# Two rounding passes of a requantisation loop moved from VectorE to GpSimd

## The chip, the cores and the metric

The kernel runs on all 8 cores of one Trainium2 chip. The metric is device time in microseconds of the slowest core. Each core computes 2 of the 16 batch rows with the same program, and nothing is exchanged between cores. In the profile the engines are PE (TensorE), DVE (VectorE), ACT (ScalarE), POOL (GpSimd) and SP (SyncE).

## The reference

The input x is [16, 2048, 1024] in float32. It is normalised over the last axis; one branch is a causal linear attention with decay, the other a quantised feed-forward block, and their product is added to x.

```
xn = layernorm(x)
s  = attention(xn)                       # q, k, v, o of width 256, decayed causal scores
h  = act_quant(xn) @ weight_quant(w1).T  # 1024 -> 4096
h  = silu(depthwise_conv1d(h, conv_w, conv_b))       # 3 taps along the sequence
y  = act_quant(h) @ weight_quant(w2).T   # 4096 -> 1024
out = x + s * silu(y)

def act_quant(x):
    scale = 127.0 / clip(max(abs(x), axis=-1), 1e-5)
    return clip(round(x * scale), -128, 127) / scale
```

The change is in act_quant(h), in its x * scale and round.

## The kernel before

**Set-up.** A core loads and quantises both weight matrices once (wquant) and keeps them in SBUF: w1q in bf16, w2q in f16. Then it goes through its 2 batch rows. In each, the 2048 positions are cut into 8 groups of GT = 256, taken from the last to the first.

**A group.** For each half of 128 positions stageA normalises, transposes and quantises the input, and stageB does the attention step. stageC multiplies the group by w1 into hs0 or hs1 (32 channel chunks of 128 partitions x 256 positions, f16). After that, tail of the group one later runs, since the convolution needs its neighbour. So tail runs 8 times in a batch row and 16 times on a core.

**The tail.** It is written in this order: (a) the convolution as small matmuls into psC and psD, with Silu on ACT back into hs (L744, L755); (b) a max tree and a min tree over the channels on DVE (L766 to L777), and per-position scales from them (L788 to L812); (c) the scales are spread over all partitions by two matmuls into psG (L827); (d) the requantisation loop, `for q in range(HC // 2)`, of 16 passes over two channel chunks each (128 x 512 elements); (e) for each half tl, 64 matmuls by w2 into psE and psF (L875), Silu on ACT, the attention output, the product with it, the sum with x, and one output DMA issued from POOL's queue (L963).

**A pass of loop (d)** has four DVE instructions. L837 multiplies hs by the scales in psG into scrf. L843 adds and subtracts 1.5 x 2^23 from scrf into g_sb. L847 adds and subtracts 1.5 x 2^52 on scrf in place. L851 forms g_sb * col(29) + scrf into hs. The constant col(29), worked out once from the engine's own arithmetic, makes the last step pick whichever of the two roundings is a real one. There is one buffer scrf and one buffer g_sb. The q loop names no other engine.

**Order and waits.** Each engine has its own queue, in the order in which the program is written. E.op increments a counter semaphore of its engine (V for DVE, G for POOL, T for PE, S for ACT) at each instruction. The program is built with strict=True: ahead of each instruction, an engine other than PE waits for its own counter to reach the number it has issued, so that an instruction starts only when the one before it has ended. Waits already made are not repeated:

```
            if (self.strict and self.ownsem is not None
                    and self.which != "tensor"):
                v0 = self.n.get(self.ownsem, 0)
                if v0 > 0 and v0 > self.waited.get(self.ownsem, 0):
                    self.eng.wait_ge(self.sems[self.ownsem], v0)
```

The first matmul behind the loop waits for its last DVE instruction, vhq:

```
                w = (use("psE0") + use("psE1h") + use("psF") + [("V", vhq)] +
                     [res.get("colsB", ("V", 0))])
```

Of the kernel before, what the change touches and what calls it, by code (L numbers as in the profile page):

```python
# [12 lines left out]
ALU = mybir.AluOpType  # L13
# [99 lines left out]
def build_nc(S=S_FULL, nbatch=NB_BATCH, strict=True, detect_races=False, limit=None):  # L113
# [102 lines left out]
    def col(i):  # L216
        return cols[:, i:i + 1]

    def schedule(E: Emit):
        n = E.n  # L220
        res = {}

        def use(key):
            return [res[key]] if key in res else []
# [7 lines left out]
        def hwaits(b):  # L232
            return [res[k] for k in
                    ("hs%d_T" % b, "hs%d_V" % b, "hs%d_S" % b) if k in res]
# [24 lines left out]
        def hap(kb, c0, nch, w=GT, off=1):  # L259
            a = hsb[kb][:, c0 * HSW + off: c0 * HSW + off + nch * HSW]  # L260
            return a.rearrange("p (a q) -> p a q", a=nch, q=HSW)[:, :, 0:w]
# [41 lines left out]
        for dst, src in casts:  # L303
            E.op("vector", lambda v, d=dst, s=src: v.tensor_copy(out=d, in_=s),
                 waits=[("DC", dc_all)])
        if "convdiag" not in DBG_SKIP:
            for idx in range(96):
# [3 lines left out]
                    waits=[("DC", dc_all)])  # L311
# [4 lines left out]
            waits=[("DC", dc_all)])  # L316
        E.op("vector", lambda v: v.tensor_scalar(
            out=col(28), in0=col(28), scalar1=2.0 ** 30, scalar2=None,
            op0=ALU.mult))
        E.op("vector", lambda v: v.tensor_scalar(  # L320
            out=col(29), in0=col(28), scalar1=-1.0, scalar2=1.0,
            op0=ALU.mult, op1=ALU.add))
        E.op("scalar", lambda s: s.activation(
            out=scal[0:1, 2:3], in_=scal[0:1, 0:1], func=AF.Sigmoid),
            waits=[("DC", dc_all)])
# [12 lines left out]
        for slot in (LND, DCN, OSC):  # L338
# [10 lines left out]
            waits=[("V", v_bc)])  # L349
# [383 lines left out]
        def tail(bi, k, base):  # L733
# [3 lines left out]
            for hc in range(HC):  # L737
                pb = hc % 2
                w = use("psCD%d" % pb) + (wh if hc == 0 else [])
                for i in range(4):  # L740
                    for kk in range(3):
# [11 lines left out]
                             waits=(w if (kk == 0 and i == 0) else []))  # L753
# [5 lines left out]
                    waits=[("T", tcv)] + (wh if hc <= 1 else []))  # L759
# [5 lines left out]
            for op2, base2 in ((ALU.max, 0), (ALU.min, 1)):  # L765
# [3 lines left out]
                    waits=(wtree if base2 == 0 else []))  # L769
# [11 lines left out]
                for tl in range(2):  # L781
                    sl = transp(scr[:, tl * 128:(tl + 1) * 128], bf="f16",
                                waits=[("V", vtree)])
# [3 lines left out]
                    if base2 == 0:  # L787
# [3 lines left out]
                            waits=[("T", ttr)] + use("colsB"))  # L791
                    else:
# [16 lines left out]
                            op0=ALU.mult, op1=ALU.mult))  # L809
# [11 lines left out]
            for t2 in range(2):  # L821
# [3 lines left out]
                    waits=[("V", vrbcols)] + use("dgt"))  # L825
# [4 lines left out]
                    waits=[("V", vdg2)] + use("psG%d" % (slb + t2)))  # L830
# [4 lines left out]
            for q in range(HC // 2):  # L835
                c0 = q * 2
                E.op("vector", lambda v, c2=c0, rp=rb_ps: v.tensor_tensor(  # L837
                    out=scr_f32[:, 0:512].rearrange(
                        "p (a q2) -> p a q2", a=2, q2=GT),
                    in0=hap(kb, c2, 2),  # L840
                    in1=rp.unsqueeze(1).broadcast_to([128, 2, GT]),
                    op=ALU.mult), waits=(wrd if q == 0 else []))
                E.op("vector", lambda v: v.tensor_scalar(  # L843
                    out=g_sb[:, 0:512], in0=scr_f32[:, 0:512],
                    scalar1=12582912.0, scalar2=12582912.0,
                    op0=ALU.add, op1=ALU.subtract))
                E.op("vector", lambda v: v.tensor_scalar(  # L847
                    out=scr_f32[:, 0:512], in0=scr_f32[:, 0:512],
                    scalar1=6755399441055744.0, scalar2=6755399441055744.0,
                    op0=ALU.add, op1=ALU.subtract))  # L850
                E.op("vector", lambda v, c2=c0: v.scalar_tensor_tensor(  # L851
                    out=hap(kb, c2, 2),
                    in0=g_sb[:, 0:512].rearrange(
                        "p (a q2) -> p a q2", a=2, q2=GT),
                    scalar=col(29),
                    in1=scr_f32[:, 0:512].rearrange(
                        "p (a q2) -> p a q2", a=2, q2=GT),
                    op0=ALU.mult, op1=ALU.add))
            res["gx"] = ("V", n["V"])
            setr("scrf", "V")  # L860
            vhq = n["V"]
# [7 lines left out]
            for tl in range(2):  # L869
                w = (use("psE0") + use("psE1h") + use("psF") + [("V", vhq)] +  # L870
                     [res.get("colsB", ("V", 0))])
                for hc in range(HC):
                    for dgrp, p2 in ((0, psE), (1, psF)):
# [8 lines left out]
                             waits=(w if (hc == 0 and dgrp == 0) else []))  # L882
                tf2 = n["T"]
                htouch(kb, "T")
                for dgrp, p2 in ((0, psE), (1, psF)):
# [5 lines left out]
                         waits=[("T", tf2), ("V", vhq)] +  # L891
# [8 lines left out]
                for i in range(2):  # L900
# [8 lines left out]
                         waits=[("T", trt)])  # L909
# [4 lines left out]
                for cc in range(2):  # L914
# [7 lines left out]
                         waits=(w if cc == 0 else []))  # L922
# [4 lines left out]
                    waits=[("T", tu)] + use("u_sb"))  # L927
# [7 lines left out]
                    waits=[("T", tut)] + use("uT_sb"))  # L935
# [3 lines left out]
                for dgrp, p2 in ((0, psE), (1, psF)):  # L939
# [25 lines left out]
                    waits=[("V", vcb)], inc=do, amt=16)  # L965
            res["xg%d" % kb] = ("DO%d" % kb, n["DO%d" % kb])

        for bi in range(nbatch):
            base = bi * S
            E.op("vector", lambda v: v.memset(S_sb[:, :], 0.0),  # L970
                 waits=use("S_sb"))
# [5 lines left out]
            for g0 in (NG - 1, NG - 2):  # L977
                if g0 < 0:
# [8 lines left out]
                    waits=use("xg%d" % bidx), inc=dx, amt=16)  # L987
                setr("xg%d" % bidx, dx)

            for g in range(NG - 1, -1, -1):  # L990
# [26 lines left out]
                if "SCOL" not in DBG_SKIP:  # L1017
                    vsc = n["V"]
                    for tl in range(2):
# [3 lines left out]
                            waits=use("dgt"))  # L1023
# [5 lines left out]
                            waits=[("V", vdg)] +  # L1029
# [5 lines left out]
                        waits=[("T", tscb)] + use("scol_sb"))  # L1035
# [4 lines left out]
                if g <= NG - 2:  # L1040
                    oth = (g + 1) % 2
                    wf = hwaits(cur) + hwaits(oth)
                    E.op("vector", lambda v, o=oth, c=cur: v.tensor_copy(
                        out=hsb[o][:, 0:HC * HSW:HSW],
                        in_=hsb[c][:, GT:HC * HSW:HSW]), waits=wf)
                    E.op("vector", lambda v, o=oth, c=cur: v.tensor_copy(
                        out=hsb[c][:, GT + 1:HC * HSW:HSW],
                        in_=hsb[o][:, 1:HC * HSW:HSW]))
                    htouch(cur, "V")
                    htouch(oth, "V")  # L1050
                    if "TAIL" not in DBG_SKIP:
                        tail(bi, g + 1, base)
                if 1 <= g <= NG - 2:
# [8 lines left out]
                        waits=use("xg%d" % bidx), inc=dx, amt=16)  # L1062
                    setr("xg%d" % bidx, dx)
            E.op("vector", lambda v: v.memset(hs0[:, 0:HC * HSW:HSW], 0.0),
                 waits=hwaits(0))
            htouch(0, "V")
            if "TAIL" not in DBG_SKIP:
                tail(bi, 0, base)
# [50 lines left out]
```

How the kernel before makes its waits and increments, by code:

```python
    def op(self, engine, fn, waits=(), inc=None, amt=1, serialize=False):  # L47
        if inc is None:
            inc = ENG2SEM[engine]
        self.total += 1
        if self.limit is not None and self.total > self.limit:
            self.n[inc] += amt
            return self.n[inc]
        if engine == "tensor" and (serialize or self.tser):
            if engine == self.which:
                v0 = self.n["T"]
                if v0 > 0 and v0 > self.waited.get("T", 0):
                    self.eng.wait_ge(self.sems["T"], v0)
                    self.waited["T"] = v0
            self.tser = serialize
        if engine == self.which:
            if (self.strict and self.ownsem is not None
                    and self.which != "tensor"):
                v0 = self.n.get(self.ownsem, 0)
                if v0 > 0 and v0 > self.waited.get(self.ownsem, 0):
                    self.eng.wait_ge(self.sems[self.ownsem], v0)
                    self.waited[self.ownsem] = v0
            for sk, v in waits:
                if v > 0 and v > self.waited.get(sk, 0):
                    self.eng.wait_ge(self.sems[sk], v)
                    self.waited[sk] = v
            inst = fn(self.eng)
            inst.then_inc(self.sems[inc], amt)
        self.n[inc] += amt
        return self.n[inc]
```

## Time and profile before

| | |
|---|---|
| median of 3 runs | 5139.29 us (5133.31 to 5140.38) |
| the profiled execution | 5140.66 us |
| its span, slowest core | 5139.1 us (the eight cores: 5122.6 to 5139.1) |
| PE busy | 1950.4 us (38%) |
| DVE busy | 2324.1 us (45%) |
| ACT busy | 402.8 us (8%) |
| POOL busy | 17.3 us (0%), 36 instructions |

No engine is busy for half of the span. A share of busy time therefore tells little here, and the stages have to be read one by one in the order of time. The span is that of the traced instructions on the slowest core; the device time of the same execution is 1.6 us more.

### The profile page before, as it was taken

What the parts mean: (1) busy time and instruction counts of PE and PEld (TensorE: products, weight loads), DVE (VectorE), ACT (ScalarE), POOL (GpSimd) and SP (SyncE); (2) the same over time, 40 slices, a digit from 0 to 9 for tenths busy, and PEclk for the clock granted to TensorE, in tenths of its full rate; (3) what the DMA queues carried; (4) which work ended last, traced back from release to release, by engine and by line L of the source; (5) the groups of instructions that cost most, each with busy time, mean ns of one, the idle gap of its engine ahead of it and who ended that gap; (6) DMA issues with size and microseconds to landing.
All of it is one profiled execution on the core that took longest, in us unless ns stands there. A gap on an engine that the chain in (4) does not pass through costs nothing.

```text
span 5139.1 us, 45903 instructions; the slowest of 8 cores (5122.6 to 5139.1 us)
## 1 busy us (share of the span) xinstructions
PE 1950.4 (38%) x14474; PEld 1178.8 (23%) x14474; DVE 2324.1 (45%) x5416; ACT 402.8 (8%) x745; POOL 17.3 (0%) x36
## 2 busy tenths in 40 slices
PE   0000015536253433345354356353443444353543
PEld 0000003314131222223132134131222223131311
DVE  4875764343534343534334543444343434434344
ACT  0000000101001010101011001001010101010110
POOL 0000000000000000000000000000000000000000
PEclk9999997666667575766676666667575767676766
DMA  4323210000000000000000000000000000000000
GB/s 129 104 93 106 72 51 1 1 17 1 17 1 5 13 1 17 1 17 1 17 1 17 17 1 1 17 1 5 13 1 17 1 17 1 17 1 17 1 9 9
DMA packets 43507, 105.54 MB, mean 21 GB/s; under 512 B 12292, under 2 KB 14468, under 8 KB 39172
## 3 DMA queue, kind: packets, MB, share of 16 engines
q1 hardware_dynamic: 38660, 85.82, 5.1%
q0 software_dynamic: 4608, 16.78, 0.8%
q8 instruction: 120, 1.97, 0.2%
q14 instruction: 119, 0.97, 0.1%
HBM read 85.80 MB, written 16.78 MB: 20 GB/s over the span
## 4 chain that ended last, share of the span: by engine, by line
DVE 41%; PE 37%; issue 11%; DMA 5%; ACT 3%; DVEq 2%; SPq 0%; ACTq 0%; POOL 0%; POOLq 0%
PE psG L254 8%; PE psE L875 5%; PE psF L875 5%; PE psA L703 5%; PE psB L703 5%; DVE sb_scr L771 4%; DVE sb_hs L851 4%; DVE sb_scrf L837 3%; PE psC L744 3%; DVE sb_g_sb L843 2%; DVE sb_scrf L847 2%; ACT sb_hs L755 2%; PE psD L744 2%; DVE sb_xg L430 2%; DMA sb_xg<-w2t 2%
## 5 line engine op out<-in xcount | busy, mean ns | idle before, releaser
L254 PE MATMUL psG<-sb_eyef,sb_g_sb 128*128 128x128 f32 x1024 | 392.4, 487 | 1211.3 <-ACT sb_g_sb L493 744.6
L875 PE MATMUL psE<-sb_w2q,sb_hs 128*128 128x512 f16 x1024 | 426.7, 417 | 730.1 <-DVE sb_hs L851 700.6
L254 PEld LDWEIGHTS psG<-sb_eyef,sb_g_sb 128*128 128x128 f32 x1024 | 256.6, 312 | 1351.9 <-issue 1351.9
L875 PE MATMUL psF<-sb_w2q,sb_hs 128*128 128x512 f16 x1024 | 424.8, 415 | 0.0
L875 PEld LDWEIGHTS psE<-sb_w2q,sb_hs 128*128 128x128 f16 x1024 | 108.3, 106 | 884.7 <-issue 786.9
L703 PE MATMUL psA<-sb_xqsT,sb_w1q 128*128 128x256 bf16 x2048 | 270.4, 290 | 0.0
L703 PE MATMUL psB<-sb_xqsT,sb_w1q 128*128 128x256 bf16 x2048 | 254.9, 280 | 0.0
L905 DVE CAST sb_Rg<-psG 128x128 bf16<-128x128 f32 x64 | 18.6, 291 | 513.9 <-PE psG L254 513.9
L703 PEld LDWEIGHTS psA<-sb_xqsT,sb_w1q 128*128 128x128 bf16 x2048 | 213.8, 104 | 34.7
L703 PEld LDWEIGHTS psB<-sb_xqsT,sb_w1q 128*128 128x128 bf16 x2048 | 206.7, 101 | 29.4
L771 DVE TENSOR_TENSOR sb_scr<-sb_scr,sb_hs 128x512 f16<-128x512 f16 x448 | 191.8, 428 | 47.8 <-DVE sb_scr L771 0.9
L766 DVE TENSOR_TENSOR sb_scr<-sb_hs 128x512 f16<-128x512 f16 x32 | 13.7, 428 | 429.9 <-ACT sb_hs L755 428.3
L851 DVE SCALAR_TENSOR_TENSOR sb_hs<-sb_g_sb,sb_cols,sb_scrf 128x512 f16<-128x512 f32 x256 | 193.1, 754 | 27.0 <-DVE sb_scrf L847 0.5
L744 PE MATMUL psC<-sb_hs,sb_convdiag 32*32 32x256 f16 x3072 | 162.8, 313 | 108.2 <-ACT sb_hs L755 72.5
L837 DVE TENSOR_TENSOR sb_scrf<-sb_hs,psG 128x512 f32<-128x512 f16 x256 | 175.8, 687 | 42.1 <-PE psG L827 16.3
L561 DVE CAST sb_xqsT<-psG 128x128 bf16<-128x128 f32 x256 | 74.7, 292 | 262.2 <-PE psG L254 262.2
L515 DVE CAST sb_xqsT<-psG 128x128 bf16<-128x128 f32 x256 | 74.7, 292 | 234.5 <-PE psG L254 229.0
L744 PE MATMUL psD<-sb_hs,sb_convdiag 32*32 32x256 f16 x3072 | 164.2, 314 | 17.4 <-ACT sb_hs L755 1.9
L755 ACT ACTIVATE sb_hs<-psC,sb_convb_sb 128x256 f16<-128x256 f32 x256 | 122.1, 477 | 603.3 <-PE psD L744 578.6
L392 PE MATMUL psG<-sb_cols,sb_onem 128*128 128x1 f32 x4 | 1.1, 348 | 440.6 <-DVE sb_cols L388 440.6
L721 DVE TENSOR_TENSOR sb_hs<-psA,sb_scol_sb 128x512 f16<-128x512 f32 x128 | 88.8, 694 | 164.4 <-PE psB L703 125.5
L887 ACT ACTIVATE sb_g_sb<-psE,sb_cols 128x512 f32<-128x512 f32 x32 | 22.0, 687 | 1692.5 <-PE psG L254 1692.5
(150 smaller groups left out, 2466.0 us busy)
## 6 DMA issues: line engine op xcount, KB each, us to landing
sb_xg<-w1t SPq DMA_DIRECT2D x32, 1024.0 KB, 5.3
sb_xg<-w2t SPq DMA_DIRECT2D x128, 256.0 KB, 2.6
sb_xg<-x SPq DMA_DIRECT2D x16, 1024.0 KB, 4.9
out<-sb_xg POOLq DMA_DIRECT2D x32, 512.0 KB, 2.9
sb_xg<-basis SPq DMA_DIRECT2D x1, 512.0 KB
sb_xg<-basisT SPq DMA_DIRECT2D x1, 512.0 KB
sb_xg<-qcT SPq DMA_DIRECT2D x1, 128.0 KB
sb_xg<-kcT SPq DMA_DIRECT2D x1, 128.0 KB
```

The costliest lines, as they stand in the source:

```text
L254: t.matmul(out=psG[:, s * 128:(s + 1) * 128], lhsT=a, rhs=idn[:, :], start=True, stop=True),
L430: v.scalar_tensor_tensor(out=f[:, s3], in0=scrf[:, 0:512], scalar=col(29), in1=f[:, s3], op0=ALU.mult, op1=ALU.add))
L703: lambda t, i2=i, h2=hc, p2=pb, s2=slot: t.matmul(out=psAB[p2][:, s2:s2 + 256], lhsT=w1q[:, i2 * H + h2 * 128: i2 * H + (h2 + 1) * 128], r ...
L721: v.tensor_tensor(out=d, in0=s3, in1=s4, op=ALU.mult),
L744: t.matmul(out=psCD[p2][32 * i2:32 * (i2 + 1), 0:256], lhsT=convdiag[32 * i2:32 * (i2 + 1), (h2 * 3 + k2) * 32: (h2 * 3 + k2 + 1) * 32], r ...
L755: E.op("scalar", lambda s, h2=hc, p2=pb: s.activation(out=hk[:, h2 * HSW + 1:h2 * HSW + 1 + GT], in_=psCD[p2][:, 0:256], func=AF.Silu, bia ...
L771: E.op("vector", lambda v, c2=c0, o3=op2: v.tensor_tensor(out=scr[:, 0:512].rearrange("p (a q) -> p a q", a=2, q=GT), in0=scr[:, 0:512].re ...
L837: E.op("vector", lambda v, c2=c0, rp=rb_ps: v.tensor_tensor(out=scr_f32[:, 0:512].rearrange("p (a q2) -> p a q2", a=2, q2=GT), in0=hap(kb, ...
L843: E.op("vector", lambda v: v.tensor_scalar(out=g_sb[:, 0:512], in0=scr_f32[:, 0:512], scalar1=12582912.0, scalar2=12582912.0, op0=ALU.add, ...
L847: E.op("vector", lambda v: v.tensor_scalar(out=scr_f32[:, 0:512], in0=scr_f32[:, 0:512], scalar1=6755399441055744.0, scalar2=6755399441055 ...
L851: E.op("vector", lambda v, c2=c0: v.scalar_tensor_tensor(out=hap(kb, c2, 2), in0=g_sb[:, 0:512].rearrange("p (a q2) -> p a q2", a=2, q2=GT ...
L875: lambda t, h2=hc, d2=dgrp, t2=tl, p3=p2: t.matmul(out=p3[:, 0:512], lhsT=hk[:, h2 * HSW + 1 + t2 * 128: h2 * HSW + 1 + (t2 + 1) * 128], r ...
```

## The change

In each pass of loop (d), the two rounding instructions L843 and L847 are issued on GpSimd with the same operands and constants. The first of them waits for the multiplication by DVE, and DVE's last instruction of the pass waits for the second.

```diff
+                vq1 = n["V"]
-                E.op("vector", lambda v: v.tensor_scalar(
+                E.op("gpsimd", lambda g: g.tensor_scalar(
                     out=g_sb[:, 0:512], in0=scr_f32[:, 0:512],
                     scalar1=12582912.0, scalar2=12582912.0,
-                    op0=ALU.add, op1=ALU.subtract))
-                E.op("vector", lambda v: v.tensor_scalar(
+                    op0=ALU.add, op1=ALU.subtract), waits=[("V", vq1)])
+                E.op("gpsimd", lambda g: g.tensor_scalar(
                     out=scr_f32[:, 0:512], in0=scr_f32[:, 0:512],
                     scalar1=6755399441055744.0, scalar2=6755399441055744.0,
                     op0=ALU.add, op1=ALU.subtract))
-                E.op("vector", lambda v, c2=c0: v.scalar_tensor_tensor(
+                gq = n["G"]
+                E.op("vector", lambda v, c2=c0, gq2=gq: v.scalar_tensor_tensor(
                     out=hap(kb, c2, 2),
                     ...
-                    op0=ALU.mult, op1=ALU.add))
+                    op0=ALU.mult, op1=ALU.add), waits=[("G", gq)])
```

## Rows read from the trace of the kernel before

**Rows 1.** Spans and granted TensorE clock of the cores and dies.

```profile
core 0: 5139.1 us, clock 0.703
core 3: 5122.6 us, clock 0.709
...
die 0 (median of its cores): 5127.2 us, clock 0.709
die 1 (median of its cores): 5129.5 us, clock 0.708
```

**Rows 2.** Waits: engine, line, releaser; us in total, times, longest us.

```profile
PE psE L875 <- DVE sb_hs L851: 700.6, 16, 44.0
```

**Rows 3.** Instruction groups of loop (d): count, busy us, mean ns, idle before.

```profile
L851 DVE SCALAR_TENSOR_TENSOR sb_hs<-sb_g_sb,sb_cols,sb_scrf 128x512 f16<-128x512 f32 x256 | 193.1, 754 | 27.0 <-DVE sb_scrf L847 0.5
...
L837 DVE TENSOR_TENSOR sb_scrf<-sb_hs,psG 128x512 f32<-128x512 f16 x256 | 175.8, 687 | 42.1 <-PE psG L827 16.3 <-DVE sb_hs L851 0.9
L843 DVE TENSOR_SCALAR sb_g_sb<-sb_scrf 128x512 f32<-128x512 f32 x256 | 109.3, 427 | 28.3 <-DVE sb_scrf L837 1.4
L847 DVE TENSOR_SCALAR sb_scrf<-sb_scrf 128x512 f32<-128x512 f32 x256 | 109.2, 427 | 27.9 <-DVE sb_g_sb L843 0.9
```

**Rows 4.** Timeline of the first tail: start us, duration us.

```profile
1029.98 0.69 DVE L837 TENSOR_TENSOR sb_scrf<-sb_hs,psG 128x512 f32<-128x512 f16 x1 [1.02 <-PE psG L827]
1030.78 0.43 DVE L843 TENSOR_SCALAR sb_g_sb<-sb_scrf 128x512 f32<-128x512 f32 x1
1031.31 0.43 DVE L847 TENSOR_SCALAR sb_scrf<-sb_scrf 128x512 f32<-128x512 f32 x1
1031.84 0.75 DVE L851 SCALAR_TENSOR_TENSOR sb_hs<-sb_g_sb,sb_cols,sb_scrf 128x512 f16<-128x512 f32 x1
1032.70 0.69 DVE L837 TENSOR_TENSOR sb_scrf<-sb_hs,psG 128x512 f32<-128x512 f16 x1
...
1072.59 0.75 DVE L851 SCALAR_TENSOR_TENSOR sb_hs<-sb_g_sb,sb_cols,sb_scrf 128x512 f16<-128x512 f32 x1
...
1073.49 0.58 PE L875 MATMUL psE<-sb_w2q,sb_hs 128*128 128x512 f16 x1 [43.61 <-DVE sb_hs L851]
```

**Rows 5.** Windows: the first tail's loop, and the matmuls behind it.

```profile
1030.00:1073.40 43.40, 0.00 (x0) 0.00 (x0) 36.70 (x64) 0.00 (x0) 0.00 (x0) 0.50 0.00 0
...
1074.00:1076.00 2.00, 2.00 (x6) 0.61 (x5) 0.00 (x0) 0.00 (x0) 0.00 (x0) 0.50 0.03 8
```

**Rows 6.** One-input passes at other rates, and the DVE's shortest, same columns as rows 3.

```profile
L379 DVE TENSOR_REDUCE sb_scrf<-sb_xg 128x4 f32<-128x512 f32 x64 | 43.9, 686 | 55.3 <-DMA sb_xg<-w2t 54.6 <-DVE sb_cols L388 0.5 <-DVE sb_cols L367 0.2
...
L489 DVE TENSOR_SCALAR sb_cols<-sb_cols 128x1 f32<-128x1 f32 x32 | 4.9, 153 | 3.4
...
L887 ACT ACTIVATE sb_g_sb<-psE,sb_cols 128x512 f32<-128x512 f32 x32 | 22.0, 687 | 1692.5 <-PE psG L254 1692.5
```

**Rows 7.** All groups of POOL.

```profile
L963 POOL DMA_DIRECT2D out<-sb_xg x32 | 17.1, 536 | 5115.9 <-DVE sb_xg L955 5075.2 <-DVE sb_hs L1064 40.7
...
L116 POOL MEMSET const-float32-1.0<- 128x1 f32 x1 | 0.1, 98 | 0.0
```

**Rows 8.** Timeline around one output DMA at the end of a tail.

```profile
1116.74 1.23 DVE L955 TENSOR_TENSOR sb_xg<-sb_xg,sb_g_sb 128x1024 f32<-128x1024 f32 x1
1118.54 0.53 POOL L963 DMA_DIRECT2D out<-sb_xg  x1 [21.98 <-DVE sb_xg L955]
```

## The prediction

> **What bounds the kernel now.** I read the spans of the cores first. The two dies lie 2.3 us apart at nearly one clock, so the execution is undisturbed and core 0, the slowest, can stand for the time [rows 1]. On the page no engine is busy for half of the span, so no engine's total decides, and the next view is that of the waits. There TensorE's first matmul by w2 (L875) waits 16 times for the last instruction of the requantisation loop, 700.6 us in total, the longest wait being 44.0 us [rows 2]. Sixteen is the number of tails on a core; the loop stands once in each with PE idle behind it.
>
> The next question is whether anything else works during that wait. The window over the first tail's loop has 64 DVE instructions and none on PE, ACT or POOL, and the DMA share is 0.00 [rows 5]. The 64 are 16 passes of four. So the loop is a stretch in which one instruction at a time runs on the whole core, and the timeline shows them end to end: L837, L843, L847, L851, and L837 again [rows 4]. The 15 passes between the L851 at 1031.84 and that at 1072.59 take 40.75 us, 2.717 us each. The four durations add up to 687 + 427 + 427 + 754 = 2295 ns [rows 3], which leaves 0.422 us for four starts, 0.105 us each. That gap is the wait of each instruction for the end of the one ahead. All 256 passes look alike: L843 and L847 have 256 instructions each at a mean of 427 ns [rows 3], and 256 passes of 2.717 us are 695 us, of the 700.6 us that PE waits [rows 2]. Everything that a pass gains or loses arrives at the end of the kernel 256 times.
>
> **The change part by part.** Removed from DVE: L843 and L847, 256 instructions each of 427 ns, with a 0.105 us start ahead of each. That is 2 x (0.427 + 0.105) = 1.064 us of a pass, or 272 us in all. If DVE were the bound beside a working POOL, these could be hidden. They are not: L843 reads what L837 of the same pass has just written, L851 needs both results, and the next L837 comes behind L851 in DVE's queue and overwrites scrf. With one scrf and one g_sb, POOL's two instructions lie exactly where DVE's two lay, and DVE stands idle meanwhile. The gain by taking work off DVE is nothing: the price is the difference between the two engines' times for the same two instructions, plus the difference in the starts.
>
> Added on the path: two TENSOR_SCALAR on POOL, of 128x512 f32 in and out, with duration P each; a start of POOL behind DVE; a start of POOL behind itself (strict order makes the second wait for the first to end); and a start of DVE behind POOL.
>
> *The duration P.* POOL computes nothing in this trace but four 128x1 MEMSETs of about 98 ns, and issues 32 DMAs at 536 ns [rows 7]. P must come from neighbours. The lower bound is built from fixed cost and rate. DVE's shortest TENSOR_SCALAR takes 153 ns, which leaves 274 ns of the 427 for 512 elements, 0.54 ns each [rows 3, 6]. POOL's smallest instruction of 98 ns [rows 7] with that same rate gives 98 + 274 = 372 ns. DVE evidently runs this shape in a fast way, since passes over as many elements elsewhere take much longer: 686 ns for a reduction with one input on DVE, 687 ns for an activation on ACT [rows 6], and 754 ns for L851 with two operations and two inputs [rows 3]. For the upper bound I take twice the ordinary pass, 2 x 686 = 1372 ns, on the grounds that rows of 128x512 within this trace differ by a factor of 1.8 (427 to 754) and POOL could lie as far again beyond the ordinary row. I choose 754 ns, the row nearest in kind: 512 float32 elements, two arithmetic operations, no fast way. The difference is 2 x (754 - 427) = 654 ns per pass, 167 us in all.
>
> The trace has no POOL arithmetic with which to judge a page's figure. The Trainium skill (GPSIMD Engine Reference, section 3.1, Elementwise — side-by-side cycle accounting) puts a tight POOL loop at about 1.8 cycles per element and gives 769 ns for 512 elements. By that figure the term would be 2 x (769 - 427) = 684 ns per pass, 175 us, and the total estimate 8 us higher than mine.
>
> *The starts.* Among DVE's own instructions a start is 0.105 us, and from the last L851 (ends at 1073.34) to the first matmul (1073.49) it is 0.15 us [rows 4]. POOL was slower in the one thing that it does here: DVE's sum ended at 1117.97 and POOL's DMA began at 1118.54, 0.57 us later [rows 8]. For each of POOL's two starts the bounds are therefore 0.105 and 0.57 us. The DMA's start may contain preparation that an arithmetic instruction hasn't, so I don't charge 0.57 twice. I charge it for the start behind DVE, which is the same kind of hand-over, and 0.105 us for POOL's start behind itself, because its MEMSET row shows a small fixed cost [rows 7]. DVE's start behind POOL I also take at 0.105 us, as behind itself. The extra is 0.57 - 0.105 = 0.465 us per pass, 119 us in all.
>
> *What else moves.* POOL's queue holds the output DMAs too. The last DMA of a tail is issued before the next tail's loop begins, and the convolution and both trees of that tail lie between; issuing a DMA takes 536 ns and is long done by then, so it costs nothing [rows 7]. Inside the loop no transfer is under way (DMA share 0.00), so nothing contends, and DVE and POOL never run together. TensorE has the lower clock, 0.50 of full speed or 1.2 GHz, during the loop and in the first 2 us behind it already [rows 5]. A longer idle time can't lower it further, and I cost that at nothing.
>
> **Sum.** 256 x (0.654 + 0.465) = 256 x 1.119 = 286 us. The profiled execution took 5140.7 us (span 5139.1 and 1.6 around it), 1.4 us above the median of the runs. 5140.7 + 286 = 5427 us, and 5425 us by the median. That is slower by 5.6%.
>
> **The rivals.**
>
> *A, POOL keeps DVE's rate.* P is then 427 ns. With the start of 0.57 us behind DVE the price is 256 x 0.465 = 119 us, or 5259 us; with ordinary starts it is 0, and the time stays at 5140 us. For it: nothing says that the same arithmetic must be slow on another engine. Against it: 427 ns is the exception among the rows of 512 elements [rows 3, 6]. The page of the skill that speaks for it is GPSIMD Engine Reference, section 4.1, Engine selection, which calls one-input elementwise work on POOL roughly line rate; no row here tests that.
>
> *B, POOL is a slow engine for arithmetic.* P is 1100 to 1372 ns and both starts are 0.57 us. At the upper ends: 2 x (1372 - 427) + 2 x 465 = 2820 ns per pass, 722 us, or 5862 us. At 1100 ns with one slow start: 1346 + 465 = 1811 ns, 464 us, or 5604 us. For it: POOL's only hand-over shown is five times an ordinary one [rows 8]. Against it: its MEMSET takes only 98 ns [rows 7].
>
> *C, faster than before.* If POOL has the fixed cost of its MEMSET and DVE's fast rate, P is 372 ns; with ordinary starts the gain is 256 x 2 x 0.055 = 28 us, or 5112 us. It decides when P plus the mean POOL start falls below 0.532 us. Against it stands the start of 0.57 us [rows 8], which alone is more than that.
>
> *D, the change doesn't do what it says,* in that DVE goes on with other work while POOL rounds. That would need the next L837 to run ahead, which the queue and the single scrf exclude; I give it no chance.
>
> **How the numbers follow.** The forecast, P of 600 to 1000 ns with one slow start or both half slow, spans 5300 to 5560 us and has 0.62. A between 5150 and 5300 us has 0.17. B above 5560 us has 0.15. No change has 0.04 and C 0.02. Two in ten may lie outside the range: it reaches down into A to 5230 and up into B to 5620 us. About 0.2% (10 us) is what a measurement of this kernel can tell from no change. Faster by more than that has 0.02, within it 0.04, slower 0.94.
>
> **What would show each step.** In the profile after, the wait of psE L875 for L851 should grow from 700.6 us to about 987 us over the same 16 times. Each pass should take 3.84 us. L837 and L851 should keep 687 and 754 ns, and POOL should have 512 TENSOR_SCALAR of about 754 ns, with DVE's idle time ahead of L851 at about 2.3 us per pass (0.57 + 0.754 + 0.105 + 0.754 + 0.105). DVE's busy time should fall by 218 us to about 2106 us while the kernel gets longer. PE's groups should keep their durations. The prediction is wrong if P or the starts are off: an error of 100 ns in P moves the time by 51 us, one of 100 ns in one start by 26 us. It is wrong in kind if the extra per pass is right but the total isn't, since then the loop isn't bare, or if L837 or L851 change their own durations.

## The result and the profile after

| | before | after |
|---|---|---|
| median of 8 runs each | 5138.12 us | 5932.72 us |
| lowest to highest | 5133.31 to 5144.83 | 5929.25 to 5934.66 |
| profiled execution, span of its slowest core | 5139.1 us | 5929.0 us |
| DVE busy | 2324.1 us | 2106.0 us |
| POOL busy | 17.3 us | 1002.1 us |

The ratio is 1.1546, with a 95% interval of 1.1533 to 1.1559: the changed kernel is 794.6 us slower. The forecast was 5425 us with a range of 5230 to 5620. The sign was right and the size was not, since the loss is 2.8 times as large as the 286 us that I had.

The waits of the changed kernel (engine, line, what it waited for; us in total, times, longest us) answer to [rows 2]:

```profile
PE psE L877 <- DVE sb_hs L853: 1491.3, 16, 93.7
DVE sb_hs L853 <- POOL sb_scrf L848: 1092.4, 256, 4.6
```

TensorE waits the same 16 times at the same place, 1491.3 us in place of 700.6. That difference of 790.7 us is the whole loss: the two profiled executions lie 5929.0 - 5139.1 = 789.9 us apart, the medians 794.6 us. Inside the loop DVE now waits in each of its 256 passes for POOL's second instruction.

The groups of instructions of the loop answer to [rows 3]:

```profile
L848 POOL TENSOR_SCALAR sb_scrf<-sb_scrf 128x512 f32<-128x512 f32 x256 | 492.0, 1922 | 40.2 <-POOL sb_g_sb L844 40.2
L844 POOL TENSOR_SCALAR sb_g_sb<-sb_scrf 128x512 f32<-128x512 f32 x256 | 491.9, 1922 | 4158.2 <-DVE sb_scrf L837 4158.2
...
L853 DVE SCALAR_TENSOR_TENSOR sb_hs<-sb_g_sb,sb_cols,sb_scrf 128x512 f16<-128x512 f32 x256 | 193.0, 754 | 1092.4 <-POOL sb_scrf L848 1092.4
...
L837 DVE TENSOR_TENSOR sb_scrf<-sb_hs,psG 128x512 f32<-128x512 f16 x256 | 176.0, 688 | 42.1 <-PE psG L827 16.4
```

The two DVE instructions that stayed have kept 688 and 754 ns. POOL's two take 1922 ns each, 4.5 times DVE's 427. The timeline of one pass (start us, duration us; it answers to [rows 4]) shows how they stand:

```profile
1033.45 0.69 DVE L837 TENSOR_TENSOR sb_scrf<-sb_hs,psG 128x512 f32<-128x512 f16 x1
1034.30 1.92 POOL L844 TENSOR_SCALAR sb_g_sb<-sb_scrf 128x512 f32<-128x512 f32 x1 [1.80 <-DVE sb_scrf L837]
1036.37 1.92 POOL L848 TENSOR_SCALAR sb_scrf<-sb_scrf 128x512 f32<-128x512 f32 x1 [0.15 <-POOL sb_g_sb L844]
1038.40 0.75 DVE L853 SCALAR_TENSOR_TENSOR sb_hs<-sb_g_sb,sb_cols,sb_scrf 128x512 f16<-128x512 f32 x1 [4.26 <-POOL sb_scrf L848]
1039.26 0.69 DVE L837 TENSOR_TENSOR sb_scrf<-sb_hs,psG 128x512 f32<-128x512 f16 x1
```

A pass takes 1039.26 - 1033.45 = 5.81 us in place of 2.717. POOL starts 0.16 us after DVE's multiplication has ended, 0.15 us after its own first instruction, and DVE starts 0.11 us after POOL. So nearly all of the 3.09 us that a pass has gained is duration: 2 x (1.922 - 0.427) = 2.99 us. The window over the first loop has PE at rest and its granted clock at 0.50, the lower level, as before, only for twice as long (the columns are those of [rows 5]: the window and its length, then busy us and instructions of PE, PEld, DVE, ACT and POOL, then PE's clock, DMA share and GB/s):

```profile
1028.40:1120.40 92.00, 0.00 (x0) 0.00 (x0) 22.37 (x31) 0.00 (x0) 61.51 (x32) 0.50 0.00 0
```

### The profile page after: what moved, and what is told of

Read it like the earlier page. It is cut to its first block, busy times and chain, and to the rows that moved or that the text cites. A ratio compares the mean times of both kernels' runs of the same rounds, so it can differ in the third digit from the quotient of the medians.

```text
span 5929.0 us, 46383 instructions; the slowest of 8 cores (5916.3 to 5929.0 us)
## 1 busy us (share of the span) xinstructions
PE 1927.2 (33%) x14442; PEld 1171.8 (20%) x14474; DVE 2106.0 (36%) x4904; ACT 402.8 (7%) x745; POOL 1002.1 (17%) x548
## 4 chain that ended last, share of the span: by engine, by line
DVE 32%; PE 31%; POOL 17%; issue 11%; DMA 4%; ACT 3%; DVEq 2%; POOLq 0%; SPq 0%; ACTq 0%
POOL sb_scrf L848 8%; POOL sb_g_sb L844 8%; PE psG L254 7%; PE psE L877 4%; PE psF L877 4%; PE psA L703 4%; PE psB L703 4%; DVE sb_scr L771 3%; DVE sb_hs L853 3%; DVE sb_scrf L837 3%; PE psC L744 2%; ACT sb_hs L755 2%; PE psD L744 2%; DVE sb_xg L430 2%; DMA sb_xg<-w2t 1%
## 5 line engine op out<-in xcount | busy, mean ns | idle before, releaser
L844 POOL TENSOR_SCALAR sb_g_sb<-sb_scrf 128x512 f32<-128x512 f32 x256 | 491.9, 1922 | 4158.2 <-DVE sb_scrf L837 4158.2
L877 PE MATMUL psE<-sb_w2q,sb_hs 128*128 128x512 f16 x1024 | 428.1, 418 | 1520.1 <-DVE sb_hs L853 1491.3
L254 PE MATMUL psG<-sb_eyef,sb_g_sb 128*128 128x128 f32 x1024 | 392.5, 487 | 1218.8 <-ACT sb_g_sb L493 753.6
L254 PEld LDWEIGHTS psG<-sb_eyef,sb_g_sb 128*128 128x128 f32 x1024 | 256.7, 312 | 1359.4 <-issue 1359.4
L848 POOL TENSOR_SCALAR sb_scrf<-sb_scrf 128x512 f32<-128x512 f32 x256 | 492.0, 1922 | 40.2 <-POOL sb_g_sb L844 40.2
L744 PE MATMUL psC<-sb_hs,sb_convdiag 32*32 32x256 f16 x3072 | 154.3, 299 | 111.7 <-ACT sb_hs L755 80.0
L744 PE MATMUL psD<-sb_hs,sb_convdiag 32*32 32x256 f16 x3072 | 155.0, 299 | 21.5 <-ACT sb_hs L755 5.8
```

The costliest lines, as they stand in the source:

```text
L254: t.matmul(out=psG[:, s * 128:(s + 1) * 128], lhsT=a, rhs=idn[:, :], start=True, stop=True),
L744: t.matmul(out=psCD[p2][32 * i2:32 * (i2 + 1), 0:256], lhsT=convdiag[32 * i2:32 * (i2 + 1), (h2 * 3 + k2) * 32: (h2 * 3 + k2 + 1) * 32], r ...
L844: E.op("gpsimd", lambda g: g.tensor_scalar(out=g_sb[:, 0:512], in0=scr_f32[:, 0:512], scalar1=12582912.0, scalar2=12582912.0, op0=ALU.add, ...
L848: E.op("gpsimd", lambda g: g.tensor_scalar(out=scr_f32[:, 0:512], in0=scr_f32[:, 0:512], scalar1=6755399441055744.0, scalar2=6755399441055 ...
L877: lambda t, h2=hc, d2=dgrp, t2=tl, p3=p2: t.matmul(out=p3[:, 0:512], lhsT=hk[:, h2 * HSW + 1 + t2 * 128: h2 * HSW + 1 + (t2 + 1) * 128], r ...
```

## The experiments

What is open after this reading is why POOL takes 1922 ns, whether hand-overs have a part in the loss, and whether POOL could carry this work at all if it ran beside DVE. Unless it says otherwise, a kernel below is the changed one with one edit, timed by a single run. The kernel before, run beside them on the same chip, took 5132 to 5139 us (5138.5, 5135.8 as the median of 7 runs, and 5132.0 on three chips).

### One rounding back on DVE

```diff
-                E.op("gpsimd", lambda g: g.tensor_scalar(
+                gq = n["G"]
+                E.op("vector", lambda v: v.tensor_scalar(
                     out=scr_f32[:, 0:512], in0=scr_f32[:, 0:512],
...
-                    op0=ALU.add, op1=ALU.subtract))
-                gq = n["G"]
+                    op0=ALU.add, op1=ALU.subtract), waits=[("G", gq)])
```

> The second rounding goes back to DVE, behind POOL's first. My theory: the loss is POOL's long duration (1.92 us for one TENSOR_SCALAR of 128x512 f32, in place of 0.427), paid once per instruction and pass. Then a pass takes 0.687 + 0.18 + 1.922 + 0.10 + 0.427 + 0.105 + 0.754 + 0.105 = 4.28 us against 5.81 after the change and 2.72 before, and the time is 5138 + 256 x 1.56 = about 5538 us. Rival: most of the loss is in handing the work over between the engines (two hand-overs a pass, which stay here); then POOL's single instruction would be shorter or the time would stay above 5700 us.

Measured: 5537.7 us. Half of the loss goes with half of POOL's instructions, though the work still changes engine twice in each pass. The remaining POOL instruction still takes 1922 ns:

```profile
L844 POOL TENSOR_SCALAR sb_g_sb<-sb_scrf 128x512 f32<-128x512 f32 x256 | 491.9, 1922 | 4301.7 <-DVE sb_scrf L837 4301.7
```

The rival of costly hand-overs falls: both hand-overs of a pass are still there, and the time is within 1 us of the sum that takes them at 0.18 and 0.10 us.

### Fewer columns: what is fixed and what is per element

First half of the columns in both POOL instructions, later a quarter:

```diff
-                    out=g_sb[:, 0:512], in0=scr_f32[:, 0:512],
+                    out=g_sb[:, 0:256], in0=scr_f32[:, 0:256],
...
-                    out=scr_f32[:, 0:512], in0=scr_f32[:, 0:512],
+                    out=scr_f32[:, 0:256], in0=scr_f32[:, 0:256],
```

> Both POOL instructions work on 256 of the 512 columns (the rounding of the other half is left out). Theory: POOL pays per element; with a fixed part of 98 ns (its MEMSET) the rate is (1922 - 98) / 512 = 3.56 ns per element, so 256 columns take 1010 ns and the time is 5932 - 256 x 2 x 0.912 = about 5465 us. Rival: a fixed price of a software instruction; then they still take 1.9 us and the time stays at 5932 us. In between, the two sizes give both parts.

Measured: 5493 us, 28 us above the estimate. The group of instructions shows where they come from:

```profile
L844 POOL TENSOR_SCALAR sb_g_sb<-sb_scrf 128x256 f32<-128x256 f32 x256 | 273.4, 1068 | 4160.8 <-DVE sb_scrf L837 4160.8
```

It takes 1068 ns, not 1010 (1069 in the second instruction). The cost goes with the number of columns, but the fixed part is larger than the MEMSET's 98 ns. Elements are counted here along the columns, as all runs have 128 partitions. From the two sizes the slope is (1922 - 1069) / 256 = 3.33 ns per element and the fixed part 216 ns. The quarter width was run to test that line on a size that it hadn't been drawn through.

> Both POOL instructions on 128 of the 512 columns (the rest isn't rounded, and DVE's sum reads scrf in place of g_sb). From the two sizes so far (1069 ns at 256 columns, 1922 at 512) the rate is 3.33 ns per element and the fixed part 216 ns: 128 columns should take 642 ns each and the time be 5932 - 256 x 2 x 1.28 = 5277 us. Rival: the line bends (a cost per block of columns, or a smallest duration); then more than 700 ns.

Measured: 5278 us, and 642 ns:

```profile
L844 POOL TENSOR_SCALAR sb_g_sb<-sb_scrf 128x128 f32<-128x128 f32 x256 | 164.2, 642 | 4162.1 <-DVE sb_scrf L837 4162.1
```

The three sizes lie on one line. Of the 1922 ns, 216 are fixed by this line, drawn on below its smallest size, and 1706 are paid per element.

### One arithmetic operation in place of two

```diff
-                    scalar1=12582912.0, scalar2=12582912.0,
-                    op0=ALU.add, op1=ALU.subtract), waits=[("V", vq1)])
+                    scalar1=1.0, scalar2=None,
+                    op0=ALU.add), waits=[("V", vq1)])
```

and the same in the second instruction.

> Both POOL instructions keep their size but do one operation (add 1.0) in place of add and subtract; the rounding is left out. Theory of the loop's fixed rate per element whatever the arithmetic: 1.92 us and 5932 us. Rival: the price is per arithmetic operation; then (1922 + 98) / 2 = 1010 ns each and about 5465 us. I give the rival 0.4.

Measured: 5703 us, between the two answers, so both were too simple.

```profile
L844 POOL TENSOR_SCALAR sb_g_sb<-sb_scrf 128x512 f32<-128x512 f32 x256 | 380.7, 1487 | 4161.5 <-DVE sb_scrf L837 4161.5
```

The second operation costs 1922 - 1488 = 434 ns (1488 is the mean of the other instruction), which is 0.85 ns per element. The rest, (1488 - 216) / 512 = 2.5 ns per element, is there with a single operation too. One operation was run at one width only, so that the fixed part is the same 216 ns, and that the 434 ns are paid per element, is an estimate.

### The values

```diff
-                    scalar1=12582912.0, scalar2=12582912.0,
+                    scalar1=1.0, scalar2=1.0,
...
-                    scalar1=6755399441055744.0, scalar2=6755399441055744.0,
+                    scalar1=1.0, scalar2=1.0,
```

> The changed kernel with 1.0 in place of both large rounding constants (nothing is rounded, all else as in the change). Theory: POOL's time doesn't depend on the values, 1.92 us each and 5932 us. Rival: the large constants make it slow (special cases in the float arithmetic of a software engine); then nearer to the one-operation or the copy duration, 0.61 to 1.49 us each, and 5260 to 5700 us.

Measured: 5931.3 us.

```profile
L844 POOL TENSOR_SCALAR sb_g_sb<-sb_scrf 128x512 f32<-128x512 f32 x256 | 492.3, 1923 | 4158.0 <-DVE sb_scrf L837 4158.0
```

The second instruction has 1924 ns, so the large constants have no part in it.

### Other instructions in the same place

A copy in place of the first rounding:

```diff
-                E.op("gpsimd", lambda g: g.tensor_scalar(
-                    out=g_sb[:, 0:512], in0=scr_f32[:, 0:512],
...
+                E.op("gpsimd", lambda g: g.tensor_copy(
+                    out=g_sb[:, 0:512], in_=scr_f32[:, 0:512]),
+                    waits=[("V", vq1)])
```

> POOL's first instruction is a tensor_copy of the same tiles (the first rounding is left out), the second stays. Theory: reading and writing on POOL is not what costs, the arithmetic of its TENSOR_SCALAR is; then the copy is far shorter than 1.92 us, say 0.5 to 0.8 us, and the time is 5932 - 256 x 1.1 to 1.4 = 5570 to 5640 us. Rival: moving an element through POOL costs 3.6 ns whatever is done to it; then the copy takes 1.9 us too and the time stays at 5932 us.

Measured: 5560.7 us.

```profile
L844 POOL COPY sb_g_sb<-sb_scrf 128x512 f32<-128x512 f32 x256 | 156.1, 610 | 4140.9 <-DVE sb_scrf L837 4140.9
```

The same tiles pass through POOL in 610 ns when nothing is calculated, so reading and writing them isn't what costs. The second instruction keeps 1923 ns. The time is some 9 us below the range that I gave.

TensorE's wait for the loop is 1150.3 us, 341 us less than after the change, or 1.33 us a pass, of which 1.31 are duration; the other 29 us between the two profiled spans lie in TensorE's own groups. The four groups of the convolution and of the matmuls by w2 are busy for 1133.5 us there and for 1163.0 us in the changed kernel, at a mean granted clock of 0.696 against 0.678. Most of that difference in the mean is only the loop, in which the clock is at 0.50 and which is 341 us shorter: over the 20 us stretches from 960 us on in which TensorE had any work, the clock is 0.674 against 0.665. The convolution's matmuls (L744) last from 263 to 417 ns in both kernels, with a mean of 288 against 299 ns, so fewer of them ran slowly. Why isn't settled, and each kernel is one execution: in the run with 1.0 for the constants, whose loop takes the time of the changed kernel's, the same four groups are busy for 1173.7 us.

Then copies in both places, as a test of the sum itself with a POOL instruction near the duration that I had forecast:

> Both POOL instructions are copies (nothing is rounded), with the waits, the hand-overs and the loop of the change. It puts a POOL instruction of 610 ns where my forecast had one of 754. If the structure of my sum is right and only the duration and the hand-overs were wrong, a pass takes 0.687 + 0.15 + 0.61 + 0.15 + 0.61 + 0.10 + 0.754 + 0.105 = 3.17 us and the time is 5138 + 256 x 0.45 = 5253 us. Rival: something beside the duration costs more once POOL stands in the loop (TensorE's clock, later stages); then 5290 us or more.

Measured: 5243.1 us, with 5132.0 us for the kernel before beside it. The waits:

```profile
PE psE L874 <- DVE sb_hs L850: 808.6, 16, 51.0
```

That is 108 us more than in [rows 2], of a loss of 111 us. The two copies take 613 ns each and a pass 3.14 us. The time is 10 us under the 5253 us that I expected: the kernel before is 6 us faster on this chip, and a pass took 0.03 us less than my 3.17, worth 8 us, which covers it to within 4 us. The structure of the sum holds.

Last, an addition with two inputs in the first place (both inputs are the same tile):

```diff
-                E.op("gpsimd", lambda g: g.tensor_scalar(
...
+                E.op("gpsimd", lambda g: g.tensor_tensor(
+                    out=g_sb[:, 0:512], in0=scr_f32[:, 0:512],
+                    in1=scr_f32[:, 0:512], op=ALU.add), waits=[("V", vq1)])
```

> POOL's first instruction is a TENSOR_TENSOR add with two inputs (scrf twice; the first rounding is left out), the second stays. The GPSIMD Engine Reference of the Trainium skill gives 2.6 cycles per element for two inputs, an estimate of 1.1 to 1.3 us for 512; by the slope of one operation seen here (2.5 ns per element) it would be 1.5 us or more. Time 5932 - 256 x (1.92 - 1.2) = 5748 us by the first, 5825 us by the second.

Measured: 5685.9 us.

```profile
L844 POOL TENSOR_TENSOR sb_g_sb<-sb_scrf 128x512 f32<-128x512 f32 x256 | 266.1, 1039 | 4152.0 <-DVE sb_scrf L837 4152.0
```

The addition of a tile takes 1039 ns, less than the addition of one constant (1488 ns). The kind of instruction decides on POOL, more than the number of inputs; what it is in TENSOR_SCALAR that costs, no run shows. The time is 62 us under the lower of my two answers, 5748 us. Of these, 41 us are the duration, 1.04 us in place of 1.2. TensorE's wait for the loop is 1265.4 us, 225.9 us less than after the change, which is 256 x 0.883 us; the other 21 us of the 247 lie outside the loop. The Trainium skill gives about 2.6 cycles per element for a tensor_tensor (GPSIMD Engine Reference, section 3.1, Elementwise — side-by-side cycle accounting), by estimate 1109 ns for 512 elements at the 1.2 GHz that it uses there; this row is 6% under it.

### POOL beside DVE

The kernel before, with one POOL instruction a pass that nobody in the loop waits for (only the Silu behind the matmuls does, by a wait that is added there):

```diff
+                E.op("gpsimd", lambda g: g.tensor_scalar(
+                    out=g_sb[:, 512:1024], in0=g_sb[:, 512:1024],
+                    scalar1=1.0, scalar2=1.0,
+                    op0=ALU.add, op1=ALU.subtract), waits=[("V", n["V"])])
                 E.op("vector", lambda v: v.tensor_scalar(
                     out=g_sb[:, 0:512], in0=scr_f32[:, 0:512],
...
```

> The kernel before, with all its arithmetic on DVE, and beside each pass one POOL TENSOR_SCALAR of 128x512 f32 on the unused half of g_sb, which no instruction of the loop waits for. It takes 1.92 us of a pass of 2.72 us. Theory: DVE and POOL don't disturb each other much, and the time stays within 10 us of 5138 us. Rival, by the rule of the Trainium skill (SBUF - State Buffer) that VectorE in a two-port mode, or with two SBUF inputs, and GpSimd take a shared port pair in turns for whole instructions: in each pass one DVE instruction waits for most of POOL's 1.92 us, or POOL's instruction is held up; at 1.9 us a pass that is 256 x 1.9 = 486 us, 5624 us, and the DVE instruction that waits shows a duration of 2 us or more. Even chances.

Measured: 5186.7 us, 51 us over the kernel before, which is neither answer: 39 us above the 5148 us up to which "not much" went, and far below 5624. The timeline of one pass:

```profile
1039.84 0.69 DVE L837 TENSOR_TENSOR sb_scrf<-sb_hs,psG 128x512 f32<-128x512 f16 x1
1040.64 0.43 DVE L847 TENSOR_SCALAR sb_g_sb<-sb_scrf 128x512 f32<-128x512 f32 x1
1040.69 2.16 POOL L843 TENSOR_SCALAR sb_g_sb<-sb_g_sb 128x512 f32<-128x512 f32 x1 [0.78 <-DVE sb_scrf L837]
1041.17 0.64 DVE L851 TENSOR_SCALAR sb_scrf<-sb_scrf 128x512 f32<-128x512 f32 x1
1041.92 0.75 DVE L855 SCALAR_TENSOR_TENSOR sb_hs<-sb_g_sb,sb_cols,sb_scrf 128x512 f16<-128x512 f32 x1
```

Only the second DVE TENSOR_SCALAR changes, from 427 to 640 ns; 256 x 0.21 is 54 us, the whole loss. The sum with two SBUF inputs keeps 754 ns although POOL is at work throughout. POOL's own instruction grows from 1.92 to 2.16 us. The engines do disturb each other, by 0.2 us each in a pass. A rule of turns for whole instructions (the Trainium skill, SBUF — State Buffer, section SBUF: two separate sides, as the expectation gives it) would have held L851 or L855 until POOL's end. The trace disagrees: L851 began 0.48 us after POOL and ended 1.04 us before it, and L855 ran its 0.75 us inside POOL's instruction.

The same with a copy on POOL:

> As the run with POOL beside, but its instruction is a copy, which moves an element every 0.8 ns in place of 3.3 ns. If DVE and POOL share accesses to SBUF, the denser stream disturbs DVE's TENSOR_SCALAR more while it lasts (0.61 us): L847 or L851 of this kernel grow by 0.2 us or more, and the time is 5138 + 256 x 0.2 to 0.4, about 5190 to 5240 us. If the 0.21 us of the earlier run were a price of POOL's start alone, it stays at about 5187 us. If only overlap in time counts, the copy is over before L851 starts and the time goes back to 5138 us.

Measured: 5179.1 us. The two rows of DVE's roundings and POOL's:

```profile
L843 POOL COPY sb_g_sb<-sb_g_sb 128x512 f32<-128x512 f32 x256 | 222.4, 869 | 4211.5 <-DVE sb_scrf L837 4211.5
...
L850 DVE TENSOR_SCALAR sb_scrf<-sb_scrf 128x512 f32<-128x512 f32 x256 | 163.9, 640 | 27.9 <-DVE sb_g_sb L846 0.9
L846 DVE TENSOR_SCALAR sb_g_sb<-sb_scrf 128x512 f32<-128x512 f32 x256 | 109.8, 429 | 28.2 <-DVE sb_scrf L837 1.4
```

DVE pays the same 0.21 us beside a copy as beside a slow TENSOR_SCALAR. TensorE's wait for the loop is 755.7 us here and 755.6 us in the run before, 55 us above [rows 2]. So neither POOL's density of accesses nor its duration sets the price. The copy itself grows from 610 to 869 ns. The run can't tell a price of POOL's start from one of any overlap, because the copy (1041.42 to 1042.29 in its trace) was still running when L850 began at 1041.93. The trace of the next kernel shows that overlap alone isn't enough.

### Work that DVE can leave to POOL

Five of the 16 passes of a tail have their two roundings on POOL, with buffers of their own (the idle half of g_sb, and xqsT, whose content is used up by then), while DVE goes through the next two passes:

```diff
             for q in range(HC // 2):
+                if q % 3 == 0 and q + 2 < HC // 2:
+                    qmul(q, bufP, wrd if q == 0 else [])
+                    qround("gpsimd", bufP, gP, [("V", n["V"])])
+                    continue
+                qmul(q, bufD)
+                qround("vector", bufD, gD)
+                qsum(q, bufD, gD)
+                if q % 3 == 2:
+                    qsum(q - 2, bufP, gP, [("G", n["G"])])
...
```

> The kernel before, but in 5 of 16 passes of each tail the two roundings run on POOL, on buffers of their own, while DVE does the next two passes whole; DVE takes the sum of the POOL pass after those. POOL needs about 0.18 + 1.92 + 0.15 + 1.92 + 0.10 = 4.3 us and DVE's two passes cover 5.43 us. If DVE and POOL don't disturb each other, 16 x 5 x 1.064 = 85 us are saved: 5053 us. If they take turns at a shared port, DVE is held for most of POOL's 3.8 us in each of the 80 cases: minus 85 plus up to 304, 5200 to 5360 us, slower than before. Even chances, as for the run with POOL beside.

Measured: 5078.2 us (median of 4 runs) against 5135.8, ratio 0.9887 with a 95% interval of 0.9870 to 0.9903. That is 1.1% less than the kernel before, a small gain and outside the noise. The timeline from one multiplication for POOL to the next:

```profile
1040.11 0.69 DVE L840 TENSOR_TENSOR sb_xqsT<-sb_hs,psG 128x512 f32<-128x512 f16 x1
...
1040.96 2.17 POOL L847 TENSOR_SCALAR sb_g_sb<-sb_xqsT 128x512 f32<-128x512 f32 x1 [3.01 <-DVE sb_xqsT L840]
1041.70 0.43 DVE L847 TENSOR_SCALAR sb_g_sb<-sb_scrf 128x512 f32<-128x512 f32 x1
1042.23 0.43 DVE L850 TENSOR_SCALAR sb_scrf<-sb_scrf 128x512 f32<-128x512 f32 x1
...
1043.28 2.03 POOL L850 TENSOR_SCALAR sb_xqsT<-sb_xqsT 128x512 f32<-128x512 f32 x1 [0.15 <-POOL sb_g_sb L847]
...
1044.41 0.43 DVE L847 TENSOR_SCALAR sb_g_sb<-sb_scrf 128x512 f32<-128x512 f32 x1
1044.95 0.64 DVE L850 TENSOR_SCALAR sb_scrf<-sb_scrf 128x512 f32<-128x512 f32 x1
1045.69 0.75 DVE L857 SCALAR_TENSOR_TENSOR sb_hs<-sb_g_sb,sb_cols,sb_scrf 128x512 f16<-128x512 f32 x1
1046.62 0.76 DVE L857 SCALAR_TENSOR_TENSOR sb_hs<-sb_g_sb,sb_cols,sb_xqsT 128x512 f16<-128x512 f32 x1 [0.17 <-DVE sb_hs L857]
1047.47 0.69 DVE L840 TENSOR_TENSOR sb_xqsT<-sb_hs,psG 128x512 f32<-128x512 f16 x1
```

Three passes take 7.36 us in place of 3 x 2.717 = 8.15. I had 7.09; the missing 0.27 us are the 0.21 us of one disturbed rounding and a start of 0.17 us in place of 0.105. Over the 80 cases that is 22 us, of the 25 us by which the time lies above my 5053. POOL ends at 1045.31 and DVE wants its result only at 1046.6, so POOL's 2.17 + 2.03 us are hidden here. The same instructions that lose 795 us in series win 58 us (5135.8 - 5078.2) when 5 of 16 passes have their roundings beside DVE.

One more thing can be read from this trace. Beside POOL's first instruction (1040.96 to 1043.13) lie two roundings of DVE whole, at 1041.70 and 1042.23, and both kept 0.43 us; of the two that begin beside its second instruction (1043.28 to 1045.31) only the later, at 1044.95, took 0.64. So a rounding isn't slowed by every overlap with POOL. What decides which one is, stays open. 0.64 us is near the 0.69 us of the ordinary rows of this size [rows 6], but that a slowed rounding loses DVE's fast way is only a guess.

### A shorter loop on DVE alone

The kernel before, with the second rounding and the choice between the two left out:

```diff
-                E.op("vector", lambda v: v.tensor_scalar(
-                    out=g_sb[:, 0:512], in0=scr_f32[:, 0:512],
+                E.op("vector", lambda v, c2=c0: v.tensor_scalar(
+                    out=hap(kb, c2, 2),
+                    in0=scr_f32[:, 0:512].rearrange(
+                        "p (a q2) -> p a q2", a=2, q2=GT),
                     scalar1=12582912.0, scalar2=12582912.0,
                     op0=ALU.add, op1=ALU.subtract))
-                E.op("vector", lambda v: v.tensor_scalar(
-                    out=scr_f32[:, 0:512], in0=scr_f32[:, 0:512],
...
-                E.op("vector", lambda v, c2=c0: v.scalar_tensor_tensor(
...
```

> The kernel before, with L847 and L851 left out of the loop and L843 writing its rounded result straight to hs in f16 (the choice between two roundings by col(29) is gone from this loop; the first is the one that counts where the engine's arithmetic is float32). Theory that everything in the loop arrives at the end 256 times: minus 256 x (0.532 + 0.859) = 356 us, 4782 us. Rival: the float32 to float16 write takes DVE off its fast rate, 0.69 us in place of 0.43, which gives back 67 us, 4849 us.

Measured: 4780.8 us (median of 4 runs) against 5135.8, ratio 0.9305 (0.9291 to 0.9319). The rounding now writes f16:

```profile
L843 DVE TENSOR_SCALAR sb_hs<-sb_scrf 128x512 f16<-128x512 f32 x256 | 110.1, 430 | 27.9 <-DVE sb_scrf L837 0.9
```

It keeps DVE's fast duration. Removing 1.39 us from a pass removes 355 us from the kernel. This version beats both kernels; it relies on DVE's arithmetic being float32, which the kernel before left open by its choice with col(29).

## Why the prediction was right in sign and wrong in size

**The loop is bare, and each microsecond of a pass counts 256 times.** Right. The wait of PE behind the loop grew by 790.7 us, and 256 x 3.09 us is 791. The version with two copies, that with one rounding, and the three widths confirm it in both directions. Two kernels had something outside the loop as well, of 29 us (one copy) and 21 us (two inputs).

**No gain from taking work off DVE.** Right. DVE's busy time fell by 218 us, as forecast, and none of it showed in the time. The run with two buffer sets shows what was missing: something for DVE to do meanwhile.

**The starts.** Forecast at 0.465 us a pass above before, by the 0.57 us that POOL's DMA needed behind DVE [rows 8]. Measured: 0.16, 0.15 and 0.11 us, together 0.10 us above three ordinary starts. That is 26 us in place of 119, an error of 93 us in the other direction. POOL's arithmetic doesn't start as late as its DMA; the prediction named that doubt and charged the DMA's start once all the same.

**The duration P: the step that failed.** The prediction says: "I choose 754 ns, the row nearest in kind: 512 float32 elements, two arithmetic operations, no fast way." Measured: 1922 ns, so the term was 2.99 us a pass in place of 0.654, or 765 us in place of 167. My upper bound of 1372 ns was also too low. It was taken from the spread of rows on other engines, and rows of DVE and ACT bound nothing on an engine whose cost is built differently: 216 ns fixed, 2.5 ns per element for the first operation and 0.85 for the second, by the estimate above. Rival B, the slow engine, was the right case, with its 0.15; even its upper end of 5862 us lay 71 us under the result, since its starts were too long by 0.83 us a pass and each P too short by 0.55. One of the bounds was also added up wrongly: with P = 600 ns and starts of 0.465 us extra the time is 5347 us, not the 5300 with which the forecast's span begins.

**The page beside it.** The Trainium skill's figure of 1.8 cycles per element, 769 ns (GPSIMD Engine Reference, section 3.1), would have given 8 us more than my number. The trace disagrees with it for this instruction by a factor of 2.5. The Trainium skill's "roughly line-rate" (the same page, section 4.1, Engine selection), which speaks for rival A, is nearest to the copy among the instructions run here (610 ns), and even that is longer than DVE's 427 ns.

**Output DMAs, the loads, TensorE's clock.** Costed at nothing, and the sum came out right: the wait behind the loop grew by 790.7 us and the profiled span by 789.9. The granted clock was 0.50 in the first loop before and after, and the first matmul behind it took 0.58 us in both. "PE's groups should keep their durations" held only roughly, and what moved nearly cancelled. The convolution's matmuls went from a mean of 314 to 299 ns and the four groups from 1178.5 to 1163.0 us, while PE's waits for ACT at L254 and L744 grew by 9.0 and 7.5 us. With the 29 us of the run with one copy this suggests that TensorE's stages can move by some tens of microseconds between kernels that differ only in this loop; no run isolates the cause.

## What to carry to other kernels

Moving an instruction to an idle engine saves nothing when its input is the last thing the old engine did and its output the next thing it needs; then the difference of the two durations counts (2.99 of the 3.09 us here) and that of the starts (0.10), and the duration should be taken from a row of that very instruction on that engine. Where no such row exists, the upper bound has to be set wide, since rows of other engines don't bound it. An engine 4.5 times slower can still help with a few passes if buffers of their own let it run beside, and it is worth asking first whether the step is needed at all.

## What the runs showed of the hardware that I had not expected

- POOL's time for 128 x n float32 elements, TENSOR_SCALAR with two operations: 642, 1069 and 1922 ns for n = 128, 256 and 512, a line of 216 ns + 3.33 ns x n. With one operation it is 1488 ns at 512.
- The same size as a copy takes 610 ns and as a TENSOR_TENSOR with two inputs (the same tile twice) 1039 ns. Adding a constant was slower on POOL than adding a tile.
- Hand-overs to and from POOL's arithmetic cost 0.11 to 0.16 us, where its DMA started 0.57 us after DVE.
- Beside a POOL instruction one DVE TENSOR_SCALAR of a pass took 0.64 us in place of 0.43, POOL's took 0.23 us more, and DVE's sum with two SBUF inputs kept its 754 ns inside POOL's instruction. Beside a copy it was the same 0.64 us. Other roundings that lay whole inside a POOL instruction kept 0.43 us.
